# New orders for the steps of all five engines, and idle transposes ahead of the first product

## The chip, the cores and the metric

The kernel runs on one core of one Trainium2 chip. The metric is the device time of the program in microseconds, the median of several runs. A core has five engines that run at the same time, each through its own list of instructions in order: TensorE (PE, matrix multiply, with weight loads shown as PEld), VectorE (DVE), ScalarE (ACT), GpSimd (POOL), and SyncE (SP), which here does nothing but issue DMA transfers. The engines wait for each other through semaphores.

## The reference

The input x is (2, 1024, 1024) in float32. What is computed:

```python
x = L0_attn_data
xn = _layernorm(x, axis=-1)
s = einsum('bsk,nk->bsn', xn, weight * block_mask) + bias      # mask: 32 x 32 blocks, a block is kept if any entry is set
coeffs = softmax((mean_s(xn) @ Wq.T) @ lora_keys.T / sqrt(128))  # one row of 8 per batch entry
g = silu(xn @ W_org.T + sum_e coeffs[e] * (xn @ lora_down[e]) @ lora_up[e])
x = x + s * g
```

## The kernel before

The 2048 rows of x are taken as 16 tiles of 128 rows, and two tiles make a pair; there are 8 pairs. Work goes in 16 groups u of products: u = 0 to 7 multiply pair u by the masked weight and leave s in DRAM (s_dram), u = 8 to 15 multiply pair u - 8 by the second weight and finish the output. The second weight differs per batch entry: it is W_org plus the low-rank product of lora_down and the scaled lora_up, and it is built on the chip in two phases "E", one ahead of u = 8 and one ahead of u = 12. From u = 3 on a group is done by seven products of half matrices instead of eight (a Strassen-like scheme), which needs sums and differences of quadrants (S and T steps) and snapshots of partial results (QS, ES).

Every fp32 operand is split in two parts, hi and lo, and a product is three matmuls per piece of the contraction, hi x hi, hi x lo and lo x hi (`triple`, L1004 to L1007). Only the first four products, P0 to P3, are made with whole fp32 operands (L1104), since the split isn't ready yet.

What each engine does, and in which order, is written out by hand in `ORDER` (from L108): five texts of words, one for each of SP, PE, ACT, DVE and POOL. A word is a kind and its numbers, and each engine's block walks through its words with one `if` per kind. The order on an engine is exactly that text, so a step that waits holds up all that stand behind it on that engine. The waits are computed from what a step needs and not from the order. The kinds that matter here:

- SP (transfers): LX, LM, LW, LI, LK, LY load x tiles, masks, weights, bias, Wq and keys. DL and DS load and store the down matrices, split. LU loads lora_up (L957), LD the split down matrices back from d_dram (L937), LE the W_org tiles (L952), LG an x pair of the second half (L903), LB an s block (L968), LR the residual x (L978), ST stores a block (L987 for s, L990 for the output). LD and LE take phase, column block and group or tile, as LD1.2.1. ST, QC and the like carry the number of the product that ends the block.
- PE: TX transposes of x, CP the mask counts spread over the partitions, P0 to P114 the products, E the products of the two phases (phase, column block, product), BP, K and G small ones. Ahead of the list stand 29 transposes of the identity (`WARM`, L1024).
- ACT: TC copies a transposed x, CA counts a mask, H, HB, U and D make the hi parts, QS and ES take snapshots, US scales lora_up, QO and QF end a block with silu, X, BA and BC belong to the layernorm.
- DVE: V, VB, VU and VD make the lo parts, SN the statistics of the first x tiles, LN normalizes (L1329), R sums rows for the mean, CB, CM and W apply the mask (L1341, L1349, L1354), EG and EA sum the tiles of the second weight (L1403, L1398), QC, QM and QR end a block: add, times s, plus x.
- POOL: a share of the same kinds.

Rings bound how far the engines can run ahead of each other: ten slots for the a operands, six banks of PSUM for sums (`acc_bank`) and two for small things, four slots `cst` for finished blocks (`CST`): a QC or QO of a block waits until the block four before it has been stored. The four slots of worg_sb and of s_in bound the loads in the same way: LE waits until the EG or EA that read the slot is done, LB until the QM is.

The waits that the prediction speaks of, cut to their lines:

```python
if c >= 2:                                     # LD: the slot is free when phase products are done
    for p in E_GROUP[g]: wait_product_E(sp, b, c - 2, p)
...
if k >= CST: dve.wait_ge(stored[k % CST], 16 * (k // CST))      # QC
```

`E_GROUP` is ((1, 2), (6, 5), (7, 4), (3,)): LD1.2.1, which loads group 1 for column block 2, waits for E1.0.6 and E1.0.5, and E1.2.6 waits for LD1.2.1.

Of the kernel before, what the change touches and what calls it, by code (L numbers as in the profile page):

```python
# [97 lines left out]
def order_of(text):  # L98
# [16 lines left out]
    LD0.0.1 LD0.1.2 LE0.0.1 LE0.1.1 LE0.1.0 LD0.0.2 RS14 LE0.0.3 LD0.3.0 LE0.1.3 ST58 LD0.1.3 LD0.2.0 ST56 LE0.0.2
    LE0.1.2 LE0.2.0 LD0.2.1 LE0.3.0 LD0.3.1 LD0.3.2 ST55 LD0.2.3 ST57 LG9.0 LE0.2.1 LD0.2.2 LB0 LB2 LE0.3.3 LE0.3.1
    LE0.2.3 LE0.2.2 RS15 LB3 LD0.3.3 LG10.0 LE0.3.2 LG9.1 LR0 LR1 LR2 LG10.1 LB1 LR3 LG11.0 LB4 ST60 LR5 ST64 LR4
    LG11.1 ST66 LB6 ST67 ST65 LB7 LR6 LB8 LB5 LB10 LB9 ST70 LR8 LR9 LR7 ST72 LG12.0 LB12 LR10 LG12.1 ST73 LU1.1.0
    LR11 LB11 LU1.1.1 ST77 LU1.7.0 ST74 LU1.7.1 LR13 LB14 LD1.0.0 LU1.3.0 LB13 LU1.3.1 ST80 ST79 LR12 LR14 LU1.2.0
# [1514 lines left out]
```

## Time and profile before

| | us |
|---|---|
| median of 3 runs | 432.4 |
| lowest and highest | 432.04, 434.46 |
| span of the profiled execution | 437.0 |
| TensorE busy in it | 417.0 |
| VectorE busy | 384.2 |
| ScalarE busy | 241.2 |
| GpSimd busy | 54.3 |

The page gives the profiled execution no time of its own besides its span, from its first instruction to its last. A time of a stretch or of an instruction below is of this one execution. A TensorE matmul of the profile lasts until its result is out, so two that follow each other overlap: their pace is read from the starts, and a hole from start to start is about 0.16 us longer than the idle time shown.

### The profile page before, as it was taken

The numbers are of one execution on the slowest core, as the hardware profiler recorded it, in microseconds if no ns is written. First come the engines' busy times: TensorE is split into PE (matmuls) and PEld (weight loads), VectorE is DVE, ScalarE is ACT, GpSimd is POOL, SyncE is SP. The second block draws the span as 40 slices with busy tenths as digits, with TensorE's granted clock in tenths as the row PEclk, the third lists the DMA queues.
The fourth block names the chain that finished last, engine by engine and source line by source line (L and its number), as shares of the span: only waits on it lengthen the run. The fifth ranks groups of instructions, "written<-read, shape, count | busy, mean of one in ns | idle before, by whom it ended". The sixth has DMA issues, their size and how long they took to land. (4 is left out here: it accounts for less than half of the span.)

```text
span 437.0 us, 6104 instructions
## 1 busy us (share of the span) xinstructions
PE 417.0 (95%) x1857; PEld 336.3 (77%) x1857; DVE 384.2 (88%) x592; ACT 241.2 (55%) x427; POOL 54.3 (12%) x61
## 2 busy tenths in 40 slices
PE   6699999999999999999989999999999899999995
...
PEclk9699999999999999999999999999999899999999
...
GB/s 304 400 397 174 142 150 301 303 220 301 270 272 284 326 202 255 353 352 333 325 302 199 95 74 244 174 375 348 315 366 336 271 44 177 59 241 230 170 232 200
DMA packets 46176, 110.51 MB, mean 253 GB/s; under 512 B 4800, under 2 KB 7104, under 8 KB 45376
## 3 DMA queue, kind: packets, MB, share of 16 engines
...
q14 instruction: 17, 0.14, 0.1%
...
## 5 line engine op out<-in xcount | busy, mean ns | idle before, releaser
L1005 PE MATMUL psA<-b_hi,a_hi 128*128 128x512 f32 (+1 forms) x444 | 173.9, 392 | 1.4 <-ACT snaps L1273 0.9
L1007 PE MATMUL psA<-b_hi,a_lo 128*128 128x512 f32 (+1 forms) x444 | 172.1, 388 | 0.0
L1006 PE MATMUL psA<-b_lo,a_hi 128*128 128x512 f32 (+1 forms) x444 | 172.0, 387 | 0.0
L1005 PEld LDWEIGHTS psA<-b_hi,a_hi 128*128 128x128 f32 x444 | 83.4, 188 | 21.1 <-ACT snaps L1273 2.2
L1007 PEld LDWEIGHTS psA<-b_hi,a_lo 128*128 128x128 f32 x444 | 83.4, 188 | 17.3
L1006 PEld LDWEIGHTS psA<-b_lo,a_hi 128*128 128x128 f32 x444 | 83.4, 188 | 16.3
L1388 DVE TENSOR_TENSOR b_lo<-b_raw,b_hi 128x512 fp32r<-128x512 f32 (+2 forms) x78 | 59.7, 790 | 0.0
L1229 ACT ACTIVATE b_hi<-b_raw 128x512 fp32r<-128x512 f32 (+2 forms) x66 | 44.8, 717 | 21.7 <-DVE b_raw L1395 7.8
L1273 ACT ACTIVATE snaps<-psA 128x512 f32<-128x512 f32 x39 | 23.0, 590 | 35.2 <-PE psA L1007 35.2
L1215 ACT ACTIVATE a_hi<-s_raw 128x512 fp32r<-128x512 f32 x52 | 31.7, 623 | 15.6 <-DVE s_raw L1379 13.9
L1388 DVE TENSOR_TENSOR a_lo<-s_raw,a_hi 128x512 fp32r<-128x512 f32 x52 | 35.1, 688 | 1.0 <-ACT a_hi L1215 0.8
L1215 ACT ACTIVATE a_hi<-xq 128x512 fp32r<-128x512 f32 x43 | 26.3, 623 | 13.6 <-PE psA L1007 8.2
L1388 DVE TENSOR_TENSOR a_lo<-xq,a_hi 128x512 fp32r<-128x512 f32 x43 | 29.3, 687 | 1.8 <-ACT a_hi L1215 1.8
L1005 PE MATMUL psA<-b_hi 128*128 128x512 f32 x64 | 25.6, 400 | 4.0 <-DMA b_hi<-d_dram 4.0
L1503 DVE TENSOR_TENSOR cst<-cst,s_in 128x512 f32<-128x512 f32 x31 | 22.4, 724 | 7.7 <-DMA s_in<-s_dram 4.8
L1471 DVE TENSOR_TENSOR cst<-psA,snaps 128x512 f32<-128x512 f32 x37 | 25.2, 687 | 2.2 <-issue 1.3
L1006 PE MATMUL psA<-b_lo,b_hi 128*128 128x512 f32 x64 | 25.6, 401 | 0.0
L1007 PE MATMUL psA<-b_hi 128*128 128x512 f32 x64 | 25.6, 400 | 0.0
L1289 ACT ACTIVATE cst<-cst 128x512 f32<-128x512 f32 x23 | 14.4, 628 | 19.1 <-DVE cst L1471 18.1
L1509 DVE TENSOR_TENSOR cst<-cst,xres 128x512 f32<-128x512 f32 x30 | 20.4, 688 | 4.3 <-DMA xres<-in_x_nat_dram 3.6
L1379 DVE TENSOR_TENSOR s_raw<-xq 128x512 f32<-128x512 f32 x23 | 15.7, 689 | 4.8 <-DMA xq<-xn_dram 2.5
L1258 ACT ACTIVATE b_raw<-psA 128x512 f32<-128x512 f32 x16 | 9.5, 596 | 17.7 <-PE psA L1007 17.7
...
## 6 DMA issues: line engine op xcount, KB each, us to landing
...
```

The source lines that it names most:

```text
L1005: nc.tensor.matmul(ps, l_hi, r_hi, start=first, stop=False, skip_group_check=True)
L1006: nc.tensor.matmul(ps, l_hi, r_lo, start=False, stop=False, skip_group_check=True)
L1007: return nc.tensor.matmul(ps, l_lo, r_hi, start=False, stop=over, skip_group_check=True)
L1215: nc.scalar.activation(a_hi[:, m % ARING, :], a_source(m), ACT.Copy).then_inc(act_hi, 1)
L1229: nc.scalar.activation(b_hi[:, hi_of.get(op, op), b_piece(s, op, pc), :], b_source(s, op, pc), ACT.Copy)\
L1273: nc.scalar.activation(snap(n), bank_of(n), ACT.Copy).then_inc(act_post, 1)
L1289: nc.scalar.activation(cst_of(n), cst_of(n), ACT.Silu).then_inc(act_post, 1)
L1379: nc.vector.tensor_tensor(s_raw[:, j - 1, :], a, b, op).then_inc(dve_S, 1)
L1388: nc.vector.tensor_tensor(lo, raw, hi.bitcast(F32), ALU.subtract).then_inc(dve_lo, 1)
L1471: nc.vector.tensor_tensor(cst_of(n), bank, snap(copied), ALU.add).then_inc(dve_post, 1)
L1503: nc.vector.tensor_tensor(cst_of(n), cst_of(n), s_in[:, j % 4, :], ALU.mult).then_inc(dve_post, 1)
L1509: nc.vector.tensor_tensor(cst_of(n), cst_of(n), xres[:, j % 4, :], ALU.add).then_inc(dve_res, 1)
```

## The change

The five texts of `ORDER` are replaced by others that hold the same words, in another order, and TensorE's has two new words, F0.30 and F1.14: 30 and 14 transposes of the identity into a PSUM bank that nobody reads, at full width and without a wait. The first stands ahead of CP0, the second ahead of P0. Where steps stand now, for those that the prediction names:

- SP, start: LY first; LW0.0 ahead of LX1; LM1 ahead of LW0.1. First phase E: LU0.2.1 and the loads before it now stand ahead of LD0.0.0; LE0.3.1 stands ahead of every LB. Second phase: LD1.1.0 ahead of LD1.0.1; LD1.3.1 and LD1.2.1 ahead of LD1.2.2; ST83 and ST84 behind the whole phase; LG13.0 far ahead of it, between LB9 and LR8.
- PE: the two F; CP1 ahead of TX1.0; CP2 ahead of P3; K behind P5; G1 inside the E phase. The products keep their order.
- ACT: among many moves, QS81 ahead of US1.7.0 and U1.1.1; QS53 behind US0.7.0; CA1.0 and CA1.1 earlier.
- DVE: LN0.0 ahead of SN2; LN2.0 and R0 between CA0.1 and CB0, SN1 behind CM0; V72 behind S11.4; in the later part QR and QC of the output ring stand at other distances.
- POOL: a few neighbours changed places.

The diff, cut to its core:

```diff
-    LX0 LX2 LM0 LX1 LX3 LW0.0 LW0.1 LM1 LX4 LW1.1 LW1.0 LM2 LM3 LI LW2.0 LK LY LX5 RS2 LW3.0 ST2 RS0 LX6 LX8 RS1 RS4
-    LX7 LT6 ST6 ST3 RS3 ST12 LX9 LT7 LT8 LX10 ST7 LX11 ST13 RS5 ST14 RS6 LT9 ST15 LX13 LX12 RS8 DL0 LX14 ST19 ST23
...
-    LE1.1.1 LE1.0.3 LD1.2.0 LE1.1.3 LE1.0.2 ST83 ST84 LG13.0 LE1.1.2 LD1.2.2 LE1.3.0 LE1.2.0 LD1.3.1 LD1.2.1 LE1.3.1
-    LE1.2.1 LD1.3.3 LB19 LD1.3.2 LE1.2.3 LE1.3.3 LB16 ST85 LE1.2.2 LD1.2.3 LB17 LE1.3.2 LR16 LG13.1 ST86 LG14.0 LR19
...
+    LY LX0 LX2 LM0 LW0.0 LX1 LM1 LW0.1 LW1.1 LX4 LX3 LW1.0 LM2 LM3 LX5 LI LW3.0 RS0 LK LW2.0 RS2 ST2 LX6 ST3 LT6 LX8
+    RS1 LX7 ST6 LX9 LX10 RS5 RS3 LX11 LT7 LT9 RS4 LT8 ST13 ST7 ST14 RS6 ST15 ST12 LX13 LX12 LT10 LX14 ST19 RS7 LT11
+    LX15 ST18 DL0 RS9 ST28 ST22 ST23 LT13 RS8 DS0.1 ST30 LT12 DS0.0 DL1 ST25 ST37 ST31 RS11 ST35 RS10 ST32 DS1.0 LT14
...
+    DS1.1 RS12 DL2 LT15 ST42 ST39 ST44 RS14 ST38 LG8.0 DS2.0 DS2.1 RS13 DL3 LG8.1 ST46 ST45 LU0.1.0 LU0.1.1 DS3.0
+    LU0.7.0 LU0.7.1 DS3.1 ST49 LU0.3.1 LD0.1.0 LU0.3.0 ST51 LU0.2.0 LE0.1.0 LU0.2.1 LD0.0.0 LE0.0.1 LD0.1.3 ST52
+    LD0.0.1 LE0.0.0 LD0.1.1 ST56 LD0.0.2 LE0.1.1 LE0.0.3 LD0.1.2 LD0.3.0 LD0.2.0 LE0.1.3 LE0.1.2 LE0.0.2 LD0.2.1
+    LD0.0.3 RS15 LD0.3.1 LE0.2.0 LE0.3.0 LD0.2.2 LG10.0 LE0.2.1 ST57 ST58 LE0.3.1 LD0.2.3 LD0.3.2 LE0.3.3 LE0.2.3
+    LE0.3.2 LE0.2.2 LD0.3.3 ST55 LB2 LG9.0 LR1 LR3 LB0 LR0 LG9.1 LB1 LB3 LR2 LG10.1 LR4 ST60 LG11.0 LB4 LB5 LR5 ST64
+    LB6 ST66 ST65 LG11.1 LR6 LR7 LB8 LG12.0 LB7 LG12.1 ST67 LR11 LR9 ST73 ST70 LR10 ST72 LB11 LB9 LG13.0 LR8 LU1.1.1
+    LB12 LU1.7.0 ST74 LB10 LU1.1.0 LU1.7.1 LR12 ST77 LR13 LB13 LD1.1.3 LU1.3.0 LB15 LR15 ST79 LD1.0.0 LU1.2.0 LU1.3.1
+    LU1.2.1 LB14 LD1.1.0 ST80 LD1.1.2 LE1.0.0 LR14 LD1.0.1 LD1.1.1 LE1.1.0 LD1.0.2 LE1.0.1 LD1.0.3 LE1.1.1 LE1.0.3
+    LD1.2.0 LE1.1.3 LE1.0.2 LD1.3.0 LE1.1.2 LE1.2.0 LE1.3.0 LD1.3.1 LD1.2.1 LE1.2.1 LD1.2.2 LE1.3.1 LD1.3.3 LE1.2.3
+    LD1.3.2 LD1.2.3 LE1.3.3 LE1.2.2 LE1.3.2 LR18 LB16 LB19 LB17 ST83 LG14.0 ST84 ST86 ST85 LR16 LB18 LG13.1 LG14.1 LR17
+    LG15.0 LR19 ST92 LR20 LB23 ST88 ST93 LG15.1 LB22 LR21 ST94 LB21 LB20 LR22 LR23 ST98 LR27 ST95 LR25 LB26 LB24 LB27
+    LB25 ST101 LB28 ST100 LR26 LB30 LR24 ST105 ST108 LB29 ST102 LR31 LR28 LB31 LR30 ST107 LR29 ST112 ST111 ST113 TS0
...
-    TX0.0 TX0.1 CP0 P0 TX1.0 TX1.1 CP1 TX2.0 TX2.1 P1 P2 CP2 TX3.0 P3 TX3.1 K P4 CP3 TX4.0 P5 TX4.1 P6 P7 P8 P9 P10
...
+    TX0.0 TX0.1 F0.30 CP0 F1.14 P0 CP1 TX1.0 TX2.0 TX1.1 TX2.1 P1 P2 CP2 P3 TX3.0 TX3.1 P4 P5 K P6 CP3 P7 TX4.0 TX4.1
...
+    QF77 QO79 US1.1.1 QF80 US1.1.0 US1.7.1 U1.1.0 QS81 US1.7.0 U1.1.1 US1.3.0 QS83 QF83 U1.5.0 U1.3.0 U1.5.1 US1.2.0
...
-    SN0 SN2 LN0.0 CA0.1 SN1 CB0 CM0 SN3 W0.1 W0.2 W0.3 LN1.1 LN2.0 LN2.1 V4 CB1 CM1 SN4 V2 V0 R1 W1.1 LN3.0 LN3.1
...
+    SN0 LN0.0 SN2 CA0.1 LN2.0 R0 CB0 CM0 SN1 W0.1 W0.2 W0.3 LN2.1 CB1 LN1.1 CM1 SN4 SN3 V0 W1.1 LN4.1 V2 VB0.0.0
...
+    QC73 QR67 V63 V68 V71 QM73 QC74 QM70 QR73 QM72 QR72 QR70 GC1 S12.3 V70 S11.2 S11.4 V72 QM74 QC77 V73 S12.1 QR74 V69
...
+    S15.2 QC101 QM95 QM98 QR98 V96 QR95 S15.4 QM101 QR101 QC102 QR100 V95 V97 QM102 QC105 S15.3 V99 V102 QM105 V98
...
@@ -1025,7 +1024,11 @@
                                  is_transpose=True)
             for st in pe_steps:
                 kind = st[0]
-                if kind == "CP":
+                if kind == "F":
+                    for _ in range(st[2]):
+                        nc.tensor.matmul(psA[:, ACC - 1, 0:P], ident[:, :], ident[:, :], start=True, stop=True,
+                                         is_transpose=True)
+                elif kind == "CP":
                     q = st[1]
                     bank = take_misc(st)
                     pe.wait_ge(pool_ready, 1)
```

## Rows read from the trace of the kernel before

**Rows 1.** The page, busy time and share of the span of each engine, instructions.

```profile
PE 417.0 (95%) x1857; PEld 336.3 (77%) x1857; DVE 384.2 (88%) x592; ACT 241.2 (55%) x427; POOL 54.3 (12%) x61
```

**Rows 2.** The page, the span in 40 slices: TensorE busy, and its granted clock.

```profile
PE   6699999999999999999989999999999899999995
...
PEclk9699999999999999999999999999999899999999
```

**Rows 3.** The view of waits of TensorE: total us, times, longest (last four causes).

```profile
PE psA L1005 <- DMA b_hi<-d_dram: 4.0, 2, 2.9
...
PE psA L1005 <- DVE b_raw L1398: 1.8, 1, 1.8
...
PE psA L1005 <- ACT snaps L1273: 0.9, 1, 0.9
PE psA L1005 <- DVE a_lo L1388: 0.5, 2, 0.3
```

**Rows 4.** The timeline of TensorE, first 24 us: start, us, [idle before].

```profile
1.57 5.70 PE L1024 MATMUL psA<-ident 128*128 128x128 f32 x29 [1.57 <-POOL ident L1522]
8.20 1.09 PE L1042 MATMUL psA<-ident,x_nat_sb 128*128 128x128 f32 x8 [0.93 <-DVE x_nat_sb L1329]
12.81 0.24 PE L1034 MATMUL psM<-bmx,sel 128*128 128x16 bf16 x4 [3.51 <-DVE bmx L1341]
15.20 6.06 PE L1104 MATMUL psA<-b_raw,xq 128*128 128x512 f32 x8 [2.15 <-POOL b_raw L1560]
...
23.03 7.03 PE L1104 MATMUL psA<-b_raw,xq 128*128 128x512 f32 x16
```

**Rows 5.** The timeline, first 26 us, VectorE and GpSimd.

```profile
7.61 0.54 DVE L1329 TENSOR_SCALAR x_nat_sb<-x_nat_sb,stat 128x512 f32<-128x512 f32 x1
...
9.52 1.22 DVE L1334 TENSOR_REDUCE cnt<-masks 128x1 f32<-128x1024 int32 x1 [1.37 <-DMA masks<-in_mask_dram]
...
14.01 1.05 POOL L1560 TENSOR_TENSOR b_raw<-b_raw,bmask 128x512 f32<-128x512 f32 x1 [0.80 <-DMA b_raw<-in_weight_dram]
...
14.92 1.89 DVE L1354 TENSOR_TENSOR b_raw<-b_raw,bmask 128x512 f32<-128x512 f32 x3
...
25.28 1.21 DVE L1368 TENSOR_REDUCE xpart<-xq 128x8 f32<-128x1024 f32 x1
```

**Rows 6.** The windows: stretch, us, busy of PE, PEld, DVE, ACT, POOL, clock, DMA.

```profile
13.00:20.00 7.00, 4.85 (x8) 2.19 (x7) 5.99 (x14) 2.83 (x5) 3.48 (x3) 0.51 1.02 423
141.57:355.92 214.35, 206.91 (x891) 166.87 (x890) 191.35 (x310) 116.10 (x206) 15.75 (x12) 0.99 0.77 268
226.00:230.00 4.00, 2.23 (x10) 1.54 (x10) 3.58 (x5) 1.27 (x3) 1.16 (x1) 1.00 1.02 389
340.00:345.00 5.00, 4.39 (x12) 3.51 (x13) 3.40 (x7) 1.69 (x4) 0.54 (x1) 0.66 0.78 274
355.92:415.79 59.87, 59.87 (x265) 49.54 (x264) 52.22 (x84) 30.87 (x56) 4.78 (x3) 1.00 0.53 169
```

**Rows 7.** The timeline, 226 to 230 us, VectorE and TensorE.

```profile
226.43 1.28 DVE L1403 TENSOR_TENSOR temp<-temp,worg_sb 128x512 f32<-128x512 f32 x1 [2.44 <-DMA worg_sb<-in_w_org_dram]
...
229.56 0.50 PE L1005 MATMUL psA<-a_hi,d_snaps 128*128 128x512 f32 x1 [1.76 <-DVE b_raw L1398]
```

**Rows 8.** The timeline of the DMA queue, 322 to 331 us.

```profile
323.43 0.91 SPq L990 DMA_DIRECT2D out_dram<-cst  x2
...
330.31 1.18 SPq L937 DMA_DIRECT2D b_hi<-d_dram  x2
```

**Rows 9.** The chain that ended last, in order of time: start, us, what.

```profile
330.94 9.53 DMA b_hi<-d_dram
```

**Rows 10.** The view of the tile d_dram, its transfers from issue to landing.

```profile
DMA to landing us min/median/max: 3.6/5.7/9.5
```

**Rows 11.** The timeline of ScalarE, 298 to 301 us.

```profile
298.88 1.32 ACT L1236 ACTIVATE a_raw<-a_raw,coef 128x512 f32<-128x512 f32 x2
```

**Rows 12.** The view of the tile out_dram, its transfers from issue to landing.

```profile
DMA to landing us min/median/max: 1.9/3.9/6.8
```

More of the change, by code:

```diff
@@ L115 @@
[L115 to L119, printed above, removed]
@@ L176 @@
-    VB1.6.2 VB1.6.3 QC64 S9.1 QC60 S9.4 QM60 V58 QC65 V56 V59 QM64 V57 S10.1 V60 QR64 QR60 QM66 V62 S10.2 QR66 V61
-    S10.3 S10.4 QM65 QC67 QR65 QM67 QR67 V63 QC70 V64 S11.1 V67 V68 S11.2 QC73 V65 QM70 QM72 QR70 V70 QM73 S11.4
-    QR72 QC74 QM74 V66 V69 QR73 QC77 QR74 QM77 QR77 V71 V75 V74 S12.3 S12.1 QM79 S12.2 QR79 QC80 V76 S12.4 V72 QM80
-    V73 QR80 UT1.1.0 UT1.1.1 VU1.1.0 VU1.1.1 UT1.3.0 QC83 UT1.3.1 QM83 UT1.2.1 QC84 QR83 UT1.2.0 VU1.5.1 QM84
-    UT1.4.0 UT1.4.1 QR84 QM85 VU1.2.0 QC86 VU1.2.1 VU1.6.1 QR85 VU1.6.0 QM86 VU1.5.0 VU1.7.1 VU1.4.0 QR86 EG1.0.0
@@ L186 @@
-    VB2.6.0 QC88 V82 S13.1 V83 VB2.6.1 VB2.6.2 S13.2 V85 QC92 V84 QM88 QR88 S14.1 S13.3 S13.4 V86 S14.2 V92 V89 QC93
-    QM92 V90 V87 QM93 V88 QR92 QR93 S14.3 QM94 V93 QC95 S14.4 V91 QC98 QR94 S15.3 QM95 S15.2 QR95 QM100 QR100 QC101
-    V97 QM101 V94 QR101 V99 QC102 QM98 V96 V98 QR98 V95 QM102 S15.4 QC105 QM105 V100 QR105 QC108 QM107 V102 V101
-    QM108 QR108 QR107 QC111 QC112 QM111 QR111 QM112 QR112 QM113 TQ0 QR113 TM0 TQ1 TR0 TM1 TR1
-    """,
-    """
-    SR0 LN0.1 SR2 SR1 W0.0 LN1.0 W1.0 SR4 SR3 W3.0 XR6 SR5 LN5.1 XR8 XR7 XR9 S3.1 XR11 XR10 S3.4 XR12 DT0.2 XR13
@@ new lines @@
+    BA14 QS33 H24 PB5.0 QS35 QO37 H28 H33 H32 PB5.1 BC14 QS36 H29 H30 H31 D1 H36 QS40 H34 H35 PB6.0 QS42 QO44 BC15 QS43
+    H39 PB6.1 GE0 D2 H37 H38 H44 QS47 H40 QS49 H42 H41 H46 QS50 D3 H43 US0.1.0 H47 US0.1.1 U0.1.1 US0.7.0 H45 QO51 QS53
+    US0.7.1 QS55 US0.3.1 US0.3.0 US0.2.0 U0.1.0 U0.5.0 U0.5.1 US0.2.1 H55 U0.6.1 U0.2.0 U0.2.1 U0.3.1 U0.6.0 QO57
+    U0.4.1 ES0.1.0 U0.4.0 ES0.0.0 H48 U0.7.1 U0.7.0 ES0.0.1 ES0.1.1 HB1.0.1 ES0.0.3 U0.3.0 ES0.1.3 HB1.0.0 HB1.2.0
+    HB1.2.1 HB1.1.0 HB1.1.1 ES0.3.0 ES0.2.0 HB1.3.1 HB1.3.0 HB1.0.2 ES0.2.1 ES0.3.1 HB1.0.3 HB1.5.0 HB1.4.1 HB1.4.0
@@ new lines @@
+    VU0.4.1 EA0.0.0 EG0.0.3 VU0.3.0 VB1.0.1 EA0.0.3 VB1.0.0 EA0.0.2 EA0.1.3 VB1.2.0 EA0.1.2 EA0.0.1 T1.0.3 VB1.1.1
+    T1.0.2 EA0.1.1 VB1.1.0 T1.1.1 EG0.2.0 EG0.3.0 VB1.2.1 EA0.3.0 EA0.2.0 T1.1.3 T1.1.2 VB1.3.0 EG0.3.1 T1.1.4 VB1.5.0
+    EG0.2.1 VB1.0.3 VB1.3.1 VB1.4.1 EG0.2.3 VB1.0.2 V49 EA0.2.3 EA0.2.2 EA0.3.3 EA0.3.2 VB1.4.0 EA0.2.1 VB1.2.2 VB1.1.3
+    EA0.3.1 VB1.1.2 V50 T1.3.1 VB1.3.2 T1.2.3 VB1.2.3 T1.2.2 T1.3.3 VB1.3.3 T1.3.2 T1.2.4 T1.3.4 VB1.4.2 VB1.4.3 V51
+    V52 V54 VB1.5.3 QC60 VB1.5.1 S9.1 VB1.5.2 V53 VB1.6.1 VB1.6.3 QC64 VB1.6.0 QM60 S9.4 VB1.6.2 QM64 QR64 S9.3 V56 V57
```

102 lines of the change are left out of this document (47 added, 55 removed).

## The prediction

> **What bounds the kernel now.** I read five views, in this order. The page's busy shares come first: TensorE is busy 417.0 us of a span of 437.0, VectorE 384.2, the others far less [rows 1]. So the question is what TensorE does in the rest, and how fast its clock runs. The slices say the second: the granted clock is full except in one slice at the start; one shorter loss is hidden in the digits of the slice at 340 us [rows 2]. The waits of TensorE after the start are few and small: 4.0 us for the loads of b_hi from d_dram in two places, 1.8 for a b_raw, 0.9 for a snapshot, 0.5 for two a_lo [rows 3]. The timeline of the first 24 us shows what stands ahead of the first product: eight transposes end at 9.3, a hole of 3.5, four tiny matmuls, a hole of 2.15, and then the first product, whose eight matmuls take 6.06 us; the sixteen behind them take 7.03, 0.43 each [rows 4]. VectorE and GpSimd show why the holes are there: the counts of the mask start when its load lands at 9.52, and the first piece of masked weights starts at 14.01 when its own load lands [rows 5]. The windows last: 0.51 of the clock between 13 and 20 us, that is nearly all at 1.2 instead of 2.4 GHz, and 0.66 between 340 and 345 [rows 6].
>
> The windows also give the size of what can be won. From 355.92 to 415.79, 264 matmuls (one more only overlaps the edge) take 59.87 us without a hole: 0.2268 each. From 141.57 to 355.92 there are 888 of the same kind (46 P of twelve and 56 E of six; the other three of the row are a G and two that overlap the edges), 201.4 us at that pace, against 214.35: 13.0 us are lost there [rows 6]. At the start the first product at half clock loses 15.20+6.06 less 8 x 0.43 from 15.20, about 2.5 us [rows 4]. The slices between show 9 throughout [rows 2], and after 356 nothing is lost. TensorE's own work plus its start and its last stores is therefore 437.0 - 13.0 - 2.5 = 421.5 us. The page gives the profiled execution no time besides its span of 437.0; the median of the runs shown is 432.4, 4.6 less, so an unprofiled execution loses about 10.9 where the profiled one loses 15.5. Work at a fixed pace can't differ, waits can.
>
> **The change, part by part.** No step is removed: all five lists hold the same steps as before, in another order, and 44 transposes are new. Their price is about 0.11 us each at full clock (8 in 1.09, in which the last one's way to its end, 0.2 to 0.3, is counted once), 0.197 at worst (29 in 5.70) [rows 4]: 3.3 and 1.5 us, or 5.9 and 2.8.
>
> *Start.* The small LY goes ahead of the first load and costs one issue, 0.4 us, on everything behind it. The mask count CA0.1 then ends near 11.15 instead of 9.52 + 1.22 = 10.74. Behind it VectorE now does LN2.0 and R0, 0.54 + 1.21 = 1.75 us [rows 5]; the 2.07 us from there to CP0 at 12.81 held SN1, of about that size, so CP0 comes near 13.2. LW0.0 is issued two loads earlier, so the 0.80 us that GpSimd waited for it [rows 5] go; W0.0 runs 13.8 to 14.85 and the first product begins at about 14.9 instead of 15.20. LN0.0 ahead of SN2 lets the first transposes end near 8.7. Fillers then run 8.7 to 12.0, inside the hole, and 13.3 to 14.85, inside the second: hidden at full clock, both just; uncovered, they cost at most 1.5 + 1.2. The holes left are 1.3 us and nothing. A hole of 1.76 us between full-speed stretches left the granted clock at 1.00 in 226 to 230 [rows 6, 7], the holes of 3.5 and 2.15 in 10 to 15 did not, so I take full clock: 2.5 us gained, between 0 and 2.5. Against it, LW0.1 now comes behind the 1 MB mask LM1, and SN1 stands ahead of W0.1 to W0.3 (1.89 us for the three [rows 5]): I charge 0.5 us inside the first product. CP2, moved ahead of P3, waits for a count that VectorE reaches after three VB0 steps: 0.4. Sum of the start: 0.3 + 2.5 - 0.5 - 0.4 = 1.9 us, bounds -0.9 and 2.8.
>
> *First correction phase, near 227.* VectorE stands 2.44 us for a worg load, and the E0.2.3 that needs its sum starts 1.76 us late [rows 7]; start to start it is 1.9, with 0.3 at E0.3.3. The load is LE0.3.1, queued behind LB0, which waits for the last stores of phase one. In the new queue LE0.3.1 stands ahead of all LB and VectorE's wait goes. Next late is EG0.2.3: it needs the snapshot behind E0.2.7, and the VectorE steps in front are as many as before, so of 2.44 us of standing all but what the snapshot claims is won. I leave 0.2 of the 2.2.
>
> *Second phase, near 340.* The group of loads LD1.3.1, LD1.2.1 is issued at 330.31, the second at 330.94, and that one lands 9.53 us later [rows 8, 9], 3.1 us too late, and TensorE restarts at half clock: nine matmuls at 0.43 instead of 0.23, 1.7 us more. In front of them in the queue were ST83, ST84 [rows 8], LG13.0 and LD1.2.2, 1.5 MB. The new order puts the stores and LD1.2.2 behind and LG13.0 some 40 us ahead, and V72, on which it waits, is moved up by 15 steps of VectorE, 9 us. What stays in front is LE1.3.0, which waits for GpSimd; so LD1.2.1 issues 0.6 us earlier and takes the median of its kind, 5.7, not the longest, 9.5 [rows 10]: it lands near 336.0, 1.4 us before TensorE needs it (340.5 less 3.1). All of 4.8 goes; at a landing of 9.5 again 0.6 would.
>
> *The rest.* LD1.1.0 now stands ahead of LD1.0.1, half a megabyte less before it: 0.8 of 1.2 us. QS81 stood on ScalarE behind six steps; two of them (a US, 0.66 [rows 11], and a U) now follow it: 0.8 of the 1.0 that P83 lost. The other 3.8 us (13.0 less 2.2, 4.8, 1.2, 1.0) are some ten gaps of 0.1 to 0.5. For each the step that was late (V56, V66, QS42, VU0.2.1, VB1.3.3, VB1.4.2) has 0.7 to 9 us less VectorE or ScalarE work in front; I take 2.7. Only QS53 goes the other way, behind US0.7.0, which waits for a load. Sum: 2.0 + 4.8 + 0.8 + 0.8 + 2.7 = 11.1. Moves that make other loads later (LD0.0.0 issued 5 us later behind LU0.2.1, with some 5.4 us to its use against a median of 5.7 [rows 10]; LD0.1.2 behind LE0.0.3) I charge with 1.5, between 0 and 6.
>
> *Total.* 437.0 - 1.9 - 11.1 + 1.5 = 425.5 us of span. Scaled to the 10.9 us that unprofiled executions lose, the same shares give 432.4 - 0.7 x 11.5 = 424.3. I forecast 425.3, 1.6% below 432.4. Nothing can go below about 421.3.
>
> Transposes as filler are where a page speaks against the change. The trace: the 29 transposes at the very start are the only work of TensorE up to then, and they take 5.70 us where 29 at the pace of the eight behind them would take 3.2 [rows 4]: the clock rose from 1.2 to 2.4 GHz between, on transposes alone. The Trainium skill, "TensorE: Matmul & The Clock Gate", section "Part 4: PE-mode transpose", says that the full clock "doesn't engage" for transpose mode, since it does not count as busy in the same way. By that rule the fillers would be idle time; by the trace they count. Here the trace speaks, and the rule's result is the first rival.
>
> **The rivals.** *The fillers don't hold the clock.* For it: the phase of whatever grants the clock differs between executions. Against it: the rise of the clock on transposes alone. The first product then takes 5.9 again, the second filler (14 at up to 0.2) overruns by 1.2: 425.3 + 2.5 + 1.2 = 429.0. *The loads are as slow as before and the holes move.* E phases run at a DMA share near 1; a landing of 9.5 instead of 5.7 at two loads that are now later gives 2 x 3.8 and one restart at half clock, 1.7: 425.3 + 9.3 - 1.5 = 433.1; with one such load 429. For it: the longest wait of the trace is of this kind. Against it: 1.5 MB less stand before it. *Slower: the output ring.* A QC may write its cst slot only when the store of four blocks before has landed, and VectorE stands in order behind it. Between QR and the QC that waits for its store there are now 6, 5, 5, 4 and 7 steps at QC67, QC74, QC98, QC102 and QC112, 27 x 0.63 = 17 us, where there were 9, 17, 8, 9 and 9, 52. ST95 even waits behind LR27 for QR101. Landings are 3.9 us in the median, 6.8 at most [rows 12], with 0.4 for the issue: 21.5 us, 4.5 of standing, which VectorE's 7.7 idle us of 355.92 to 415.79 alone cover [rows 6]; or 36, 19 of standing, 11.3 uncovered: 436.6. It decides from a landing of about 4.5, and the kernel is slower than before from about 6.4. *The order does not do what it says*, because the unprofiled executions don't have the holes of this profile: then only the start's 1.9 is left, 430.5.
>
> **How the numbers follow.** A measurement of this kernel tells 0.5%, 2.2 us, from no change. Forecast 0.60; fillers 0.05; loads 0.16 (half of it with one slow load); ring 0.07; holes not there 0.12. Faster by over 0.5% means below 430.2: 0.60 + 0.05 + 0.08 + half of the 0.12, since 430.5 lies at the edge, make 0.79. Within: 0.08 + 0.06 = 0.14. Slower: 0.07. The range goes from 421.8, almost the floor, to 431.0; the forecast's own is 422.5 to 428.5.
>
> **What would show it.** After: first product of 8 matmuls in about 3.9 us and a clock of 1.00 between 10 and 30 us (fillers right); no wait for b_hi over 0.5 us at the third pair of E1 and no half clock near 335 (queue right); no wait of VectorE for worg_sb near 222; waits of VectorE for out_dram at QC74, QC98, QC102 without a wait of TensorE after them. Wrong would be the prediction if TensorE has a wait over 2 us anywhere past the first product, or if the clock falls before it.

## The result, and the profile after

The changed kernel takes 465.7 us (463.13 to 468.21, 4 runs), the kernel before beside it 433.43 (432.04 to 436.66, 4 runs): 1.0752 times as long, 95% interval 1.0706 to 1.0799. The profiled execution of it took 466.74 us with a span of 464.9: an execution's time is 1.8 us more than its span. The forecast was 425.3. Of the kernels further down only lr8b has a slow profiled execution (468.92 us at a granted clock of 0.973, median 462.08), so of its profile little is used.

The page after, which answers to [rows 1, 2]: the busy line, and TensorE and its granted clock in 40 slices.

```profile
PE 429.5 (92%) x1901; PEld 343.2 (74%) x1901; DVE 394.6 (85%) x592; ACT 243.9 (52%) x429; POOL 64.9 (14%) x61
...
PE   8999899979999999898898998988999989999892
...
PEclk9999989989999999999899999998999999999998
```

TensorE is 12.5 us busier (44 transposes and several restarts at half clock), VectorE 10.4 with the same 592 instructions, and GpSimd 10.6 with the same 61. There is no one hole: eleven slices between the first and the last say 8 or 7, where, behind the start, two did. The waits of TensorE (total us, times, longest) [rows 3]:

```profile
PE psA L1004 <- DVE a_lo L1391: 7.9, 8, 2.6
PE psA L1004 <- DVE b_raw L1401: 5.1, 3, 3.3
PE psA L1004 <- ACT snaps L1276: 3.2, 3, 1.5
PE psA L1004 <- ACT psA L1150: 3.1, 1, 3.1
PE psA L1004 <- DVE b_lo L1391: 2.8, 3, 1.5
PE psM L1045 <- DVE x_nat_sb L1332: 2.1, 1, 2.1
```

No wait for b_hi is left, which was the largest of before. Some twenty small ones stand in its place, by this view most of them for VectorE (the longest, the 3.3 us under b_raw, was in truth for a load; it is followed back below). The start itself did what was forecast; timeline of TensorE, first 24 us, and two windows [rows 4, 6]:

```profile
7.93 1.21 PE L1045 MATMUL psA<-ident,x_nat_sb 128*128 128x128 f32 x8
8.98 3.44 PE L1029 MATMUL psA<-ident 128*128 128x128 f32 x30
12.50 0.24 PE L1037 MATMUL psM<-bmx,sel 128*128 128x16 bf16 x4
12.60 1.73 PE L1029 MATMUL psA<-ident 128*128 128x128 f32 x14
14.28 4.13 PE L1107 MATMUL psA<-b_raw,xq 128*128 128x512 f32 x8
```

```profile
13.00:20.00 7.00, 7.00 (x40) 4.20 (x38) 6.31 (x16) 3.68 (x7) 3.71 (x3) 1.00 1.02 416
...
141.57:355.92 214.35, 199.30 (x850) 159.62 (x850) 184.63 (x296) 114.36 (x200) 14.39 (x9) 0.98 0.77 266
```

The clock is at 1.00 (2.4 GHz) where it was 0.51. The second line is the long window of [rows 6]: 850 matmuls in it instead of 891. Where the time then goes shows best as a table: start of a product in us, in the kernel called fill (the old orders with only the idle transposes, whose profiled span of 430.5 is a usual one), and in the changed kernel.

| | P8 | P12 | P24 | P42 | E0.0.1 | P59 | P81 | E1.0.1 | P87 | P114 | last store's issue |
|---|---|---|---|---|---|---|---|---|---|---|---|
| fill | 46.1 | 57.8 | 91.8 | 142.1 | 190.4 | 230.7 | 291.3 | 308.9 | 349.4 | 423.1 | 428.1 |
| changed | 45.5 | 60.3 | 98.5 | 153.4 | 202.9 | 246.8 | 314.9 | 333.4 | 376.2 | 453.6 | 462.6 |
| later by | -0.6 | 2.6 | 6.6 | 11.3 | 12.5 | 16.1 | 23.6 | 24.5 | 26.8 | 30.5 | 34.5 |

Every stage adds to it and nothing is won back. The windows from P4 to P87 of fill and of the changed kernel say how full the engines are (us, busy of PE, PEld, DVE, ACT, POOL):

```profile
33.98:349.44 315.46, 309.89 (x1378) 253.31 (x1378) 292.25 (x431) 186.67 (x331) 37.87 (x39) 1.00 0.76 263
```

```profile
31.60:376.21 344.61, 321.82 (x1396) 258.89 (x1394) 302.27 (x431) 193.16 (x340) 47.55 (x38) 0.98 0.70 240
```

VectorE runs the same 431 instructions in both. In fill it is busy 93% of the stretch, nearly as full as TensorE with 98%. In the changed kernel it is busy 10.0 us longer and stands 42.3 us instead of 23.2. These two, 10.0 and 19.1, are the 29.1 us. The same sum can be made for TensorE (11.9 us busier, 17.2 more of standing), so it says where time is spent and not yet which engine leads.

One hole, followed back. Timelines of SyncE's queue, VectorE, ScalarE and TensorE, 66 to 99 us, a fence for each:

```profile
67.82 0.85 SPq L907 DMA_DIRECT2D xn_dram<-xq  x2
...
77.17 0.81 SPq L883 DMA_DIRECT2D xq<-in_x_t_dram  x2
```

```profile
82.20 1.23 DVE L1366 TENSOR_TENSOR xq<-xq,bc 128x1024 f32<-128x1024 f32 x1 [3.54 <-DMA xq<-in_x_t_dram]
...
89.23 1.22 DVE L1366 TENSOR_TENSOR xq<-xq,bc 128x1024 f32<-128x1024 f32 x1 [1.35 <-DMA xq<-in_x_t_dram]
```

```profile
91.75 1.15 ACT L1218 ACTIVATE a_hi<-xq 128x512 fp32r<-128x512 f32 x2 [6.36 <-DVE xq L1367]
...
97.82 0.58 ACT L1150 ACTIVATE psA<-bias_sb 128x512 f32<-128x512 f32 x1
```

```profile
98.45 0.50 PE L1004 MATMUL psA<-b_hi,a_hi 128*128 128x512 f32 x1 [3.12 <-ACT psA L1150]
```

Read from the bottom: P24 waits for PB3.0 on ScalarE, which was put behind H17; H17 stands 6.36 us for the N8 of VectorE; VectorE had stood 3.54 us for the load LT7 and 1.35 for LT8; LT7 waited on SyncE until the store RS3 had landed, and RS3 was put behind LX9, LX10 and RS5 and issued at 68.3 instead of 62.2. Four texts have a share in it.

The largest hole, 3.30 us at E0.0.3, is not what the view of waits calls it. Timelines of TensorE and of SyncE's queue, and the view of the tile d_snaps for the load issued at 214.73 alone, a fence for each:

```profile
222.68 0.76 PE L1004 MATMUL psA<-a_hi,d_snaps 128*128 128x512 f32 x1 [3.30 <-DVE b_raw L1401]
```

```profile
214.73 0.78 SPq L936 DMA_DIRECT2D d_snaps<-d_dram  x1
```

```profile
DMA to landing us min/median/max: 7.9/7.9/7.9
```

E0.0.3 waits for two things, the sum EA0.0.3 of VectorE and the load LD0.0.3. The sum was done at 218.70, before TensorE had ended the product in front (219.38). The load landed at 222.59, and TensorE started 0.09 us behind it. In the old text LD0.0.3 stands directly behind LD0.0.0 (issued at 181.97 in the kernel before, at 179.83 in fill) and there is no hole; in the new one it stands eighteen words behind LD0.0.0. In all nine kernels below that run this stretch in the new order (os50, xnfix, pb3, lr8, lr8b, ring, six, after_s, all_s) E0.0.3 starts 0.09 us behind the landing of LD0.0.3, after a hole of 1.5 to 3.0 us. None of them moves this word back, so what it costs in time is not shown.

### The profile page after: what moved, and what is told of

It is laid out like the page before. It is cut to its first block and busy times, and to the rows that moved or that the text cites. A ratio compares the mean times of both kernels' runs of the same rounds, so it can differ in the third digit from the quotient of the medians.

```text
span 464.9 us, 6194 instructions
## 1 busy us (share of the span) xinstructions
PE 429.5 (92%) x1901; PEld 343.2 (74%) x1901; DVE 394.6 (85%) x592; ACT 243.9 (52%) x429; POOL 64.9 (14%) x61
## 3 DMA queue, kind: packets, MB, share of 16 engines
q1 hardware_dynamic: 46144, 110.12, 68.3%
## 5 line engine op out<-in xcount | busy, mean ns | idle before, releaser
L1004 PE MATMUL psA<-b_hi,a_hi 128*128 128x512 f32 (+1 forms) x444 | 177.1, 399 | 16.9 <-DVE a_lo L1391 6.9
L1004 PEld LDWEIGHTS psA<-b_hi,a_hi 128*128 128x128 f32 x444 | 84.5, 190 | 40.6 <-issue 8.0
L1005 PEld LDWEIGHTS psA<-b_lo,a_hi 128*128 128x128 f32 x444 | 84.6, 191 | 16.2
L1391 DVE TENSOR_TENSOR b_lo<-b_raw,b_hi 128x512 fp32r<-128x512 f32 (+2 forms) x78 | 62.4, 819 | 0.5 <-ACT b_hi L1232 0.5
L1391 DVE TENSOR_TENSOR a_lo<-xq,a_hi 128x512 fp32r<-128x512 f32 x43 | 32.5, 761 | 1.5 <-ACT a_hi L1218 1.5
L1506 DVE TENSOR_TENSOR cst<-cst,s_in 128x512 f32<-128x512 f32 x31 | 21.5, 704 | 11.3 <-DMA s_in<-s_dram 5.9
L1004 PE MATMUL psA<-b_hi 128*128 128x512 f32 x64 | 25.2, 393 | 0.0
L1006 PE MATMUL psA<-b_hi 128*128 128x512 f32 x64 | 24.9, 390 | 0.0
L1573 POOL TENSOR_TENSOR b_raw<-b_raw,worg_sb 128x512 f32<-128x512 f32 x3 | 5.2, 1742 | 108.9 <-DMA worg_sb<-in_w_org_dram 99.2
L1371 DVE TENSOR_REDUCE xpart<-xq 128x8 f32<-128x1024 f32 x16 | 19.2, 1211 | 0.0
```

Source lines behind the costliest of these rows:

```text
L1004: nc.tensor.matmul(ps, l_hi, r_hi, start=first, stop=False, skip_group_check=True)
L1005: nc.tensor.matmul(ps, l_hi, r_lo, start=False, stop=False, skip_group_check=True)
L1006: return nc.tensor.matmul(ps, l_lo, r_hi, start=False, stop=over, skip_group_check=True)
L1371: nc.vector.tensor_reduce(xpart[:, t, :], x_tile(t // 2, t % 2).rearrange("p (k r) -> p k r", r=P), AX.X, ALU.add).then_inc(dve_R, 1)
L1391: nc.vector.tensor_tensor(lo, raw, hi.bitcast(F32), ALU.subtract).then_inc(dve_lo, 1)
L1506: nc.vector.tensor_tensor(cst_of(n), cst_of(n), s_in[:, j % 4, :], ALU.mult).then_inc(dve_post, 1)
```

## The experiments

In the ratios below, against the kernel before run beside them, an interval is about 0.004 to either side, so two kernels are told apart by 0.006 (2.6 us). Kernels are listed by question.

**Were the idle transposes good by themselves?** fill:

```diff
-    TX0.0 TX0.1 CP0 P0 TX1.0
+    TX0.0 TX0.1 F0.30 CP0 F1.14 P0 TX1.0
```

> The kernel before with nothing but the two groups of idle transposes, 30 ahead of the first mask count and 14 ahead of the first product. Theory A (the transposes hold the clock): the first product takes 3.9 to 4.2 us instead of 6.06, at a granted clock of 1.00, and the time is 433.4 - 2.2 = 431.2, if nothing else is late. Rival (only the new order of the start, with its shorter holes, keeps the clock): the first product is at half clock again, 433.4 or up to 1 us more. Second rival (the clock is won but the steps behind the first product wait for their masked weights): first product at full clock, time 433.

433.0 us, ratio 1.0030 (1.0003 to 1.0056), so 1.3 us slower if anything. The first product took 3.9 us and what follows it (TX1.0) starts 2.9 us earlier than before. At E0.2.7 the lead is 0.07: 1.0 went in a wait for kqs at G1 (184.6), 1.1 in a wait for b_hi at 222.1, the rest in small ones. The transfers and VectorE do not come earlier because TensorE does. A gain at the start is worth nothing here, so even the forecast's right part held no time.

**In which part of the orders does the loss lie?** Four kernels change from one set of orders to the other at a moment: each engine's text is the steps that had started by then in the profile of the first, and behind them all others in the second's order. ns50 begins with the new order, the others with the old.

> New orders for every step that starts in the first 50 us (the fillers among them), the old order for all that is left. Theory A (the loss is made after 50 us, by steps that stand in order behind a step that became late; the start itself is good): the new kernel is 2.7 us ahead at P8, nothing behind it is changed, so the lead stays: 433.4 - 2.7 = 430.7, between 429.5 and 432.5. Rival B (the early start itself does the harm: everything downstream wants its loads and GpSimd's results 2.7 us earlier than they can come): holes appear near 58 and 98 us as in the changed kernel and it comes out at 434 to 445. Rival C (output ring): 430.7 as A.

> The mirror image: old orders for all that starts in the first 50 us, without fillers, and the new order for the rest. Theory A: the changed kernel lost 2.7 + 27.9 = 30.6 us from P8 to its end, and all of that is in the new order: 433.4 + 30.6 = 464, between 460 and 467. Rival B (the early start does the harm): the loss is much smaller, below 445. Rival C (output ring alone): 437 to 442, since only the last 60 us are disturbed.

> Old orders for all that starts in the first 220 us of the kernel before, the new order for the rest. In the changed kernel TensorE stood 11.7 us late before the first E phase and 27.9 at the end. Theory A (a chain of head-of-line waits in every stage): the last part costs 27.9 - 11.7 = 16 by itself, 449, between 444 and 453, and TensorE has waits of 1 to 3 us in 220 to 350. Rival C (output ring): 437 to 442, with waits only behind 360 us. Rival D (the last part is only bad because it starts late and out of step): near 433, or below by the removed holes of the second E phase, 429.

> Old orders for all that starts in the first 345.5 us of the kernel before, the new order for the rest: the output ring is tested alone, with an undisturbed start. The rival of the prediction: QC102 and its neighbours stand for their stores, slower than before by 0 to 4 us, and by 11 if landings are long. From the changed kernel's trace: the part behind P87 lost 8 us there (shift 19.7 at E1.2.3, 27.9 at the end). Theory A (each stage adds its share, the last one too): 431.8 + 4 to 8 = 436 to 440. Rival D (the last stage only suffers because VectorE came late to it): 431 to 433.

ns50: 438.82 us, 1.0166 (1.0124 to 1.0208). os50: 460.71, 1.0666. os220: 453.8, 1.0526. os345: 439.22, 1.0178 (1.0131 to 1.0225). So the first 50 us in the new order, with the old behind them, cost 7, where I had expected them to be the good part, and what lies behind 345 costs 7.7, behind 220 22.7, behind 50 28.8. A change between two orders makes a hole of its own (in ns50 2.7 and 1.2 us at TX5, in os220 one of 6.5 at E0.2.3, where VectorE stood 6.4 for a worg tile), so these are not shares. The 7 of ns50 say little of the first 50 us themselves: TensorE is 0.7 us ahead of fill at P8, 6.3 behind at P24 and 7.2 at P87, so the loss is made around the change of orders. The other three show that what lies behind 50, 220 and 345 us costs time with an undisturbed start, and that no single part is the whole cause. os345 isolates the rival of the output ring. Waits of VectorE in os345 from 380 us on:

```profile
DVE cst L1475 <- DMA out_dram<-cst: 5.0, 3, 3.8
DVE cst L1471 <- DMA out_dram<-cst: 3.8, 1, 3.8
```

None of these 8.8 us for stores is in fill, though VectorE stands 3.4 at QC111 there too, for a snapshot of TensorE's result, so not all of them are loss. QC102 stands 3.8 us for ST95, which was put behind LR27, as the rival said; QC111 stands 3.8 for ST102, which the rival did not name. TensorE's P114 is 3.3 us later than in fill, the end 6.1.

**Is each hole the end of one chain (theory A), or does VectorE's fullness make them (rival B)?** Repairs of the changed kernel. xnfix and pb3 cut the chain shown above at its two ends:

```diff
-    RS1 LX7 ST6 LX9 LX10 RS5 RS3 LX11 LT7 LT9 RS4 LT8
+    RS1 LX7 ST6 RS3 RS4 LX9 LX10 RS5 LT7 LX11 LT9 LT8
```

> The changed kernel with four words of SyncE's text moved and nothing else: RS3 and RS4 (the stores of the normalized x halves 3 and 4) directly behind ST6, ahead of LX9; LT7 ahead of LX11; LT8 behind LT9. In the changed kernel RS3 is issued at 68.3 us and lands at 77.1, LT7 waits for it, lands at 82.2, and VectorE stands 3.5 us for it at N7 and 1.4 at N8; ScalarE stands 6.4 at H17, PB3.0 is behind it, and TensorE has its 3.1 us hole at P24 and 1.5 more at P25. Theory A (each hole is the end of one chain that starts with a step put too late in an in-order text, and time lost so early is not won back later): the two VectorE waits and the hole at P24 are gone, 4.6 us, to the end: ratio to the kernel before 1.075 - 0.0107 = 1.064. Rival B (VectorE is simply saturated in this stage, the waits are where it shows; or later holes give the gain back): the hole at P24 shrinks but the ratio stays between 1.070 and 1.080.

```diff
-    H17 H13 H16 BA10 BA11 HB0.3.0 H15 H14 H20 H18 PB3.0
+    PB3.0 H17 H13 H16 BA10 BA11 HB0.3.0 H15 H14 H20 H18
```

> The changed kernel with one word of ScalarE's text moved: PB3.0 (the bias of block 3.0 into its PSUM bank) from behind H18 to ahead of H17, where it no longer stands behind the step that waits 6.4 us for VectorE's N8. Theory A, in its strict form (only the order on ScalarE keeps P24 waiting): the 3.1 us hole at P24 goes, but H17, H13 and H16 stay as late as they are, so a part comes back as waits for the a operands: gain 1 to 3 us, ratio 1.069 to 1.073. Rival (the operands of P24 and P25 are late too, and PB3.0 is only the last of several late steps): no gain, ratio 1.075, with a wait of TensorE for a_hi, a_lo or b_lo in the place of psA.

xnfix: 461.76, 1.0692 (1.0655 to 1.0730). VectorE's 3.54 us at N7 shrink to this:

```profile
79.87 1.23 DVE L1367 TENSOR_TENSOR xq<-xq,bc 128x1024 f32<-128x1024 f32 x1 [0.61 <-ACT bc L1190]
```

The hole at P24 is gone and the stretch P12 to P24 is 2.6 us shorter, not 4.6, and 2.6 us is what the end keeps; the wait at P81 grew from 2.56 to 3.74. pb3: 462.94, 1.0719 (1.0673 to 1.0764), 1.4 us, with new waits of 1.10 for snaps and 1.56 for psA at 101.9 and 106.7 in place of the 3.12. The chain is right; each repair returns about half of its hole. Neither result alone stands clear of its uncertainty.

**Did the praised move of LG13.0 do harm, and is VectorE's wait at QR74 a cause?**

```diff
-    ST67 LR11 LR9 ST73 ST70 LR10 ST72 LB11 LB9 LG13.0 LR8       (changed kernel)
+    ST67 LR11 LR9 ST73 ST70 LR10 ST72 LB11 LB9 LR8 LG13.0       (lr8)
+    ST67 LR8 LR11 LR9 ST73 ST70 LR10 ST72 LB11 LB9 LG13.0       (lr8b)
```

> The changed kernel with one word of SyncE's text moved: LG13.0 from ahead of LR8 to behind it. The prediction praised LG13.0 for standing 40 us ahead of the second E phase; in the changed kernel's trace it waits for V72 (306.3 us), the residual load LR8 behind it is issued at 307.5 and lands at 313.45, VectorE stands 3.0 us for it at QR74, V69 and V76 are behind that step, and TensorE has a hole of 2.56 us at P81 and restarts at half clock. Theory A (one chain that begins in SyncE's text): VectorE's wait and the hole at P81 go, and the half clock behind it: 2.56 + 1.5 = 4.1 us, to the end: ratio 1.075 - 0.0095 = 1.0657, between 1.063 and 1.070. Rival B (VectorE is saturated, a wait taken from it comes back at the next step): ratio 1.072 to 1.078.

> The changed kernel with LR8 moved ahead of LR11 in SyncE's text. Moving LG13.0 alone brought nothing, since LR8 stands behind LR11 and LR9 too: SyncE is parked 7 us, from 294.5 to 301.1, at LR11, which waits for QR73, and then at LR9, which waits for QR70, while LR8's own slot is free from 294.1 on (QR67). Theory A: LR8 lands near 299, VectorE's 3.0 us at QR74 go, and the hole of 2.5 us with its half clock at P81: ratio 1.075 - 0.0085 = 1.0665, between 1.063 and 1.070. Rival B (V69 and V76 are late for want of VectorE's time, and the wait moves to another step): 1.072 to 1.078.

lr8: 464.51, 1.0760 (1.0717 to 1.0802), nothing. The wait is where it was:

```profile
312.01 0.69 DVE L1513 TENSOR_TENSOR cst<-cst,xres 128x512 f32<-128x512 f32 x1 [2.95 <-DMA xres<-in_x_nat_dram]
```

My diagnosis was wrong. In the timeline of SyncE's queue of the changed kernel nothing is issued between these two lines:

```profile
294.09 0.34 SPq L989 DMA_DIRECT2D out_dram<-cst  x1
301.14 2.34 SPq L977 DMA_DIRECT2D xres<-in_x_nat_dram  x2
```

SyncE is parked for 7 us at LR11, which waits for QR73, with LR8 nine words behind it. lr8b takes LR8 ahead of it: 462.08, 1.0650 (1.0586 to 1.0713), 4.4 us, and QR74 starts at 311.34 without a wait. The time agrees with theory A, but the interval is wide; and TensorE, which no longer waits at P81, stands 3.9 us at P83 for a snapshot in that execution, so a new wait in another place, as rival B has it, is not excluded.

**The output ring.**

```diff
-    LR23 ST98 LR27 ST95 LR25 LB26 ... LB30 LR24 ST105 ST108 LB29 ST102 LR31
+    LR23 ST98 ST95 LR24 LR27 LR25 LB26 ... LB30 ST105 ST108 ST102 LB29 LR31
```

> The changed kernel with three words of SyncE's text moved in its last part: ST95 ahead of LR27, LR24 directly behind ST95 (it stood ahead of ST105), ST102 ahead of LB29. In the changed kernel QC102 stands 3.8 us until ST95's store has landed, which was issued behind LR27; LR24 is issued at 441.75 behind LB30, so QR102 on GpSimd runs at 444.8, ST102 is issued at 447.8 and QC111 stands 3.9 us; QR111 stands 1.8 for LR29, issued last. Theory A: QC102 and QC111 stand under 1 us and the stretch from TensorE's last product to the end shrinks from 9.0 us (453.57 to 462.58, starts of P114 and of TS1) to the 5.1 us that the old order has: 4 us, ratio 1.066, between 1.063 and 1.070. Rival (the last blocks are bound by the landings of some 15 transfers issued together, whatever their order): ratio 1.072 to 1.076.

462.0, 1.0691 (1.0654 to 1.0728): 2.6 us of the 4. QC102's 3.8 us are gone, QC111 still stands 2.5, and two waits have grown, from 1.5 to 3.3 for s_in at QM102 and from 1.8 to 2.8 for xres at QR112. From P114 to the last issue it is 8.1 us, not 9.0; most of the gain lies ahead of P114.

**Is there a common cause?** Summed over the VectorE instructions that lasted longer than the shortest of their form, the excess is 12.8 us in the changed kernel, 3.0 in the kernel before, 2.4 in fill, and each such instruction lies beside one of GpSimd. The timeline of the changed kernel at 290 us:

```profile
289.87 0.68 DVE L1382 TENSOR_TENSOR s_raw<-xq 128x512 f32<-128x512 f32 x1
290.12 1.59 POOL L1568 TENSOR_TENSOR s_raw<-xq 128x512 f32<-128x512 f32 x1 [25.23 <-DVE a_lo L1391]
290.47 1.79 DVE L1391 TENSOR_TENSOR a_lo<-xq,a_hi 128x512 fp32r<-128x512 f32 x1
```

V66 starts 0.35 us after GpSimd's S11.3 and lasts 1.79 instead of 0.68: it ends 0.55 us after S11.3 has. V7, VB1.1.1, VB1.1.3, VB2.2.3 and QR108 end 0.55 us after theirs in the same way. after_s and before_s take that contact away:

```diff
-    nc.gpsimd.tensor_tensor(s_raw[:, j - 1, :], a, b, op).then_inc(pool_S, 1)
+    nc.gpsimd.memset(s_raw[:, j - 1, :], 0.0).then_inc(pool_S, 1)
```

and so in T, EG and QR102, 17 steps in all (the texts below say 18).

> The changed kernel, but the 18 GpSimd steps S, T, EG and QR102 don't add or subtract two tiles: each writes zeros to its output tile instead (EG and QR to 16 columns of it), with the same waits and signals, so the numbers computed are no longer the reference's. In the changed kernel VectorE's instructions last 12.8 us longer in all than the shortest of their form (15 of them, every one beside a GpSimd instruction), against 2.4 in the old order with the idle transposes; 8.6 of the 12.8 lie beside these 18 steps (the rest beside a W, an LN and an XR step). VectorE is the engine that is busy 303 of 345 us between P4 and P87. Theory A' (a third of the loss is VectorE being held while GpSimd adds): the excess falls to 4 us or less, and 5 to 9 us of time go: ratio 1.075 - 0.016 = 1.059, between 1.054 and 1.064. Rival (the held instructions stand where VectorE would have stood anyway): the excess falls and the ratio stays above 1.068.

> The same edit in the kernel before, as the measure of what else it brings (GpSimd's results come up to 1 us sooner): the same 18 steps write zeros. There VectorE's excess is 3.0 us, 2.7 of it beside these steps. Theory A': at most 2.7 us less, most of it hidden or in the last 40 us: ratio 0.995 to 1.000. If it falls as much as the changed kernel does, the gain of that one says nothing of the order: rival, ratio below 0.99.

after_s: 459.84, 1.0619 (1.0575 to 1.0663): 5.7 us less, excess 2.7 us instead of 12.8. before_s: 430.4, 0.9977 (0.9950 to 1.0003), excess 0.3. Window from P4 to P87 of after_s:

```profile
32.32:372.75 340.43, 319.01 (x1395) 257.61 (x1394) 295.29 (x431) 193.12 (x340) 33.19 (x38) 0.98 0.70 242
```

VectorE is busy 7.0 us less there and the stretch is 4.2 us shorter. So 5.7 less the 1.0 that the edit brings without the new order, 4.7 us, are put down to VectorE being held by GpSimd (the 5.7 is known to 2.8, the 1.0 to 1.1; GpSimd's results also come sooner, which before_s measures only in the old order). The Trainium skill has the mechanism in "SBUF — State Buffer", section "SBUF: two separate sides": a VectorE instruction with two SBUF inputs and a GpSimd instruction that reads SBUF contend for a shared pair of ports, an exclusive lock, and who comes second is fully blocked. The trace agrees, with the 1.79 above; the trace of before had such an instruction too (QM95, 1.78 us beside S15.1), and I did not weigh it.

**Do the parts add?** six has the moves of xnfix, lr8, ring and pb3 and LN5.0 ahead of V10; all_s has those too, with lr8b's in place of lr8's, and after_s's edit.

> The changed kernel with all repairs together, ten words moved: those of xnfix (RS3, RS4, LT7, LT8), of lr8 (LG13.0), of ring (ST95, LR24, ST102), PB3.0 ahead of H17 as in pb3, and LN5.0 ahead of V10 on VectorE (its place of before; TensorE's first hole, 2.1 us at TX5.0, waits for it). Theory A (separate chains, each with its own cause, nothing wins back lost time): the gains add: 2.6 (xnfix, measured) + 1.4 (pb3, measured) + 2.1 + 4.1 + 4 = 14 us of 32: ratio 1.043, between 1.038 and 1.050. Rival B (a common cause, VectorE's saturation): less than half of that sum, ratio above 1.057.

> The changed kernel with every repair that brought something at once: RS3, RS4, LT7, LT8; PB3.0; LN5.0; ST95, LR24, ST102; LR8 ahead of LR11; and the 18 GpSimd steps that write zeros instead of adding (S, T, EG, QR102, so the numbers are not the reference's). If the parts are separate they add: 1.0584 (six) - 0.010 (lr8b) - 0.013 (after_s) = 1.035, between 1.030 and 1.041, and some 15 of the 32 us are left in many small waits. If they share VectorE's time (what one frees another had already freed), it is above 1.045.

six: 457.78, 1.0584 (1.0541 to 1.0628): 7.2 us instead of 14. all_s: 451.75, 1.0448 (1.0408 to 1.0487): 13.1 instead of 17. The 14 was made of the sizes of holes. What xnfix, pb3, ring and lr8 had measured one by one, 2.6, 1.4, 2.6 and nothing, is 6.6, so in six the gains add; what fell short is a hole's size as the measure of its worth. For all_s the sum of six, lr8b and after_s is 7.2 + 4.4 + 5.7 = 17.3, and the 4 us missing are no more than the uncertainty of that sum. 19 of the 32 us are not accounted for by a cause that I removed. In six TensorE still waits 7.4 us for a_lo in seven places, and 1.5 at E0.0.3 for LD0.0.3; that other late steps stand behind each one repaired, with VectorE this full, is my reading and not tested.

**What is the change worth if only its good parts are taken?** mix has the old orders, the idle transposes, LE0.3.1 and LE0.3.3 ahead of LB0, and in the second phase:

```diff
-    LE1.0.2 ST83 ST84 LG13.0 LE1.1.2 LD1.2.2 LE1.3.0 LE1.2.0 LD1.3.1 LD1.2.1 LE1.3.1 LE1.2.1 LD1.3.3 LB19
+    LE1.0.2 LE1.1.2 LE1.3.0 LE1.2.0 LD1.3.1 LD1.2.1 LD1.2.2 ST83 ST84 LE1.3.1 LE1.2.1 LD1.3.3 LG13.0 LB19
```

> The old orders with the three parts of the change that its trace showed to work, and nothing else of it: the two groups of idle transposes; LE0.3.1 and LE0.3.3 ahead of LB0; LD1.2.2, ST83 and ST84 behind LD1.2.1, and LG13.0 behind LD1.3.3. Theory A: the transposes bring 2.9 us at the start, which were given back in 184 to 222 us; the waits for b_hi in the second E phase (0.6 and 1.4 us in the trace with the transposes alone, 4.0 in the one of the kernel before) and for b_raw in the first (1.8 in the kernel before, none with the transposes alone) go: 433.0 - 2 = 431, between 429.5 and 432.5, so no change against the kernel before, or up to 0.5% faster. Rival (the transfers of an E phase are bound by their total, not by their order): 433, with a wait for b_hi in another place.

> The kernel mix with three more words moved: G1 on TensorE behind P58 and GA1 on VectorE ahead of UT0.1.1 (TensorE waits 1.3 us for kqs at G1 in mix, and VectorE stands 1.6 us at UT0.1.1 while GA1 is behind it), and QS81 on ScalarE ahead of US1.7.0 (1.2 us of waiting for its snapshot at P83, with 1.4 us of US steps in front). Theory A: both holes go, 1.3 + 1.0 to 1.2 us, and nothing takes their place: 0.9992 - 0.0055 = 0.994, about 429.4 us, a kernel faster than before by just over what can be told from no change. Rival (what TensorE wins it waits for at the loads of the E phases, which do not come earlier, as with the idle transposes alone): 0.998 to 1.000.

mix: 431.63, 0.9992 (0.9970 to 1.0014). mix2: 430.15, 0.9940 (0.9919 to 0.9961), the fastest of these kernels, 2.9 us under the 433.02 of the kernel before beside it (2.6 by the ratio). Its granted clock and its larger waits behind the start:

```profile
PEclk9999999999999999999999999999999999999999
```

```profile
PE psA L1005 <- ACT snaps L1277: 1.1, 2, 0.7
PE psA L1005 <- DMA b_hi<-d_dram: 1.0, 1, 1.0
...
PE psA L1005 <- DMA d_snaps<-d_dram: 0.5, 1, 0.5
```

The wait for kqs is gone and of the one for snaps 0.4 is left at P83 (0.7 is new at 184.5). Two words added and nine moved, each with an eye on one hole, did what new orders for all 1,457 words did not.

## Why the prediction was wrong

*Start* (14.9, then 1.9 us gained): the mechanism was right and more so than said, 14.28 and full clock. P8 starts at 45.5, in the profile of before at 48.3. The first rival, that transposes don't hold the clock, is out: the granted clock is 1.00 through both groups. The sentence of the Trainium skill beside that rival ("TensorE: Matmul & The Clock Gate", "Part 4: PE-mode transpose"), that the full clock does not engage for them, does not hold in this kernel. What I did not ask is whether anything behind wanted TensorE earlier; fill says no.

*First correction phase* (2.0 us): LE0.3.1 ahead of LB0 did take VectorE's 2.44 us there. But E0.0.3 now has a hole of 3.30, the largest of the run, for LD0.0.3, which the same new queue put eighteen words behind LD0.0.0.

*Second phase* (4.8 us): right in kind. No wait for b_hi is left. Yet E1.0.1 to P87 takes 2.2 us longer than in fill, now for a_lo and b_raw. And the size was wrong: the 4.8 belonged to the one profiled execution; fill waits 1.9 us for b_hi in its second phase. The 437.0 of that execution was the largest mistake in the base: other executions of the kernel before have spans near 429.9, so only some 8 us were ever to be won, not 15.5. I scaled for it (10.9) and not far enough, the more so as I set a span of 437.0 beside times of executions, which are 1.8 us longer than their spans: 437.0 is 6.4 us above the median run and not 4.6, which leaves 9.1 of the 15.5.

*The rest* (0.8 + 0.8 + 2.7): for every step that was late before I counted what stood in front of it in the new text. That is the wrong half of the steps.

**The step that failed** is the one that charged the steps made later: "Moves that make other loads later ... I charge with 1.5, between 0 and 6". In net it measured 34 (the table's last column, which has what the moves won in it too). I looked for steps that became later only in the two E phases, near holes that the profile showed, and even there named LD0.0.0 and LD0.1.2 and passed over LD0.0.3, at which TensorE then stood 3.30 us. But between 24 and 220 us the profile of before shows next to no hole of TensorE [rows 2], with VectorE busy 191 of 214 us from 141.57 on [rows 6]: that was not slack, it was an order in which everything came just in time, and hundreds of words were moved in it. RS3, PB3.0, LN5.0, LR8 and LR24 had no row among mine, because before they cost nothing. In the very line in which I praised LG13.0 for standing 40 us ahead, LR8 had gone behind LR11, and I passed over it. And no term held GpSimd at all ("a few neighbours changed places"): other VectorE instructions stand beside its 17 two-tile steps, though its own order hardly changed, and that alone was about 4.7 us (known to 3), by the difference of after_s and before_s.

*The output ring*, the rival on the slower side, had 0.07. It was right in mechanism (a 3.8 us stand at QC102 for ST95 behind LR27) and wrong in its condition: the table has 7.7 us behind P87 and os345 7.7 in all (5.1 of them behind P87 in its profile), with landings of 3.8 us in os345's median, as short as before [rows 12]. For such landings I had nothing uncovered, and 11.3 us only for landings of 6.8. It did not need slow landings, only the queue. I had counted the steps between QR and QC, 4 at QC102 where before there were 9, and then let VectorE's idle time elsewhere in the stretch pay for them: idle time behind a late step does not shorten it. The last part is a quarter of the loss.

The test I had written down, a wait over 2 us of TensorE past the first product, was met four times (2.08, 3.12, 3.30, 2.56).

How far the cause is shown: that the orders behind the start cost the time, in several parts, is shown by os50, os220 and os345; which steps cost it is shown for 13 of the 32 us, and stays open for the rest.
